# Turning the next block's query input by VectorE and DRAM transfers in place of TensorE, and two query products by halves of the tokens

## The reference

```python
x = x + jnp.tanh(g_xattn[0]) * xattn(_layernorm(x), ctx_1024, Wq, Wk, Wv, Wo)
x = x + jnp.tanh(g_ffn[0])   * ffn(_layernorm(x), W_r, W_k, W_v, mu_r, mu_k)
# xattn: Q = q @ Wq.T, K = c @ Wk.T, V = c @ Wv.T, softmax(Q K^T / sqrt(32)) V @ Wo.T
# ffn:   xr, xk = mixes of x and x of the token before; sigmoid(xr @ W_r.T) * (relu(xk @ W_k.T)**2 @ W_v.T)
```

## Time and profile before

| | us |
|---|---|
| median of 3 runs | 1389.31 |
| lowest and highest | 1386.89, 1389.38 |
| the profiled execution, its own time | 1387.71 |
| its span in the trace | 1386.0 |
| TensorE busy | 1349.9 |
| VectorE busy | 1037.6 |
| ScalarE busy | 779.3 |
| GpSimd busy | 598.7 |

### The profile page before, as it was taken

How to read it: one execution, slowest core, us unless ns; L and a number is a source line. 1 busy time by engine, 2 the same in 40 slices (tenths; PEclk the granted TensorE clock), 3 DMA queues, 4 the chain that set the end, 5 groups by cost and what they waited for, 6 DMA issues and landing times.

```text
span 1386.0 us, 28131 instructions
## 1 busy us (share of the span) xinstructions
PE 1349.9 (97%) x9484; PEld 989.5 (71%) x9484; DVE 1037.6 (75%) x1938; ACT 779.3 (56%) x1457; POOL 598.7 (43%) x802
## 2 busy tenths in 40 slices
PE   7999999999999999999999999999999999999998
PEld 5666776777767677776777767677776777767677
DVE  6777777786877868777786877868777786877763
ACT  7745637465473645637465473645737465473633
POOL 7524345353443535345353443525344343443534
PEclk9999999999999999999999999999999999999999
DMA  9421101212111121202112111121202112111011
GB/s 304 151 57 47 59 23 66 57 53 75 53 37 38 61 68 53 64 19 73 47 53 75 53 43 32 61 68 53 67 16 76 45 53 75 53 48 28 31 47 39
DMA packets 97563, 83.88 MB, mean 61 GB/s; under 512 B 47872, under 2 KB 62720, under 8 KB 97536
## 3 DMA queue, kind: packets, MB, share of 16 engines
q1 hardware_dynamic: 97536, 83.54, 19.6%
HBM read 57.75 MB, written 20.71 MB: 57 GB/s over the span
## 4 chain that ended last, share of the span: by engine, by line
PE 80%; ACT 9%; DVE 8%; issue 2%; DMA 0%; ACTq 0%; DVEq 0%
PE g_bank L1278 45%; PE g_bank L1441 7%; PE o_bank L1388 7%; PE s_bank L1362 4%; PE d_bank L1394 4%; ACT s_bank L722 3%; ACT pq L721 3%; PE s_bank L1338 3%; PE s_bank L1372 2%; PE d_bank L1284 2%; DVE buf L921 2%; ACT buf L627 2%; DVE o_bank L1065 1%; PE o_bank L1284 1%; DVE d_bank L1065 1%
## 5 line engine op out<-in xcount | busy, mean ns | idle before, releaser
L998 DVE TENSOR_TENSOR pq<-s_bank,pq 128x512 f16<-128x512 f32 x320 | 220.2, 688 | 72.0 <-ACT s_bank L722 71.2
L994 DVE TENSOR_REDUCE mm<-s_bank 128x3 f32<-128x462 f32 (+1 forms) x384 | 198.6, 576 | 89.0 <-PE s_bank L1338 89.0
L721 ACT ACTIVATE pq<-s_bank 128x512 f16<-128x512 f32 x320 | 192.3, 601 | 93.9 <-PE s_bank L1366 93.9
L1441 PE MATMUL g_bank<-buf,WkT 128*128 128x512 f32 x720 | 189.9, 410 | 5.7 <-DVE buf L921 4.0
L722 ACT ACTIVATE s_bank<-s_bank 128x512 f32<-128x512 f32 x320 | 194.7, 608 | 0.0
L1278 PE MATMUL g_bank<-xnT,WqT 128*128 128x512 f32 x756 | 194.4, 402 | 0.0
L1278 PE MATMUL g_bank<-WoT,buf 128*128 128x512 f32 x768 | 193.5, 401 | 0.0
L509 POOL TENSOR_TENSOR buf<-place,buf 128x512 fp32r<-128x512 f32 x64 | 82.7, 1293 | 235.7 <-ACT buf L627 235.7
L1278 PE MATMUL g_bank<-WrT,buf 128*128 128x512 f32 x744 | 184.1, 396 | 0.0
L1278 PE MATMUL g_bank<-WvT,buf 128*128 128x512 f32 x708 | 174.5, 395 | 0.0
L1278 PEld LDWEIGHTS g_bank<-WrT,buf 128*128 128x128 f32 x744 | 137.2, 188 | 39.7 <-issue 10.8
(11 more groups left out here) (168 smaller groups left out, 2121.8 us busy)
## 6 DMA issues: line engine op xcount, KB each, us to landing
xa<-in_x SPq DMA_DIRECT2D x64, 256.0 KB, 3.6
x<-in_x SPq DMA_DIRECT2D x64, 256.0 KB, 2.7
out<-x SPq DMA_DIRECT2D x48, 256.0 KB, 2.0
place<-x SPq DMA_DIRECT2D x16, 256.0 KB, 2.4
out<-place SPq DMA_DIRECT2D x16, 256.0 KB, 2.0
k_all<-k_scratch SPq DMA_DIRECT2D x15, 256.0 KB, 2.8
k_low<-k_scratch SPq DMA_DIRECT2D x15, 256.0 KB, 2.9
v_main<-v_scratch SPq DMA_DIRECT2D x15, 256.0 KB, 2.8
```

The lines of the kernel that those rows point to most:

```text
L721: nc.scalar.activation(pq[:, n, HI, :], bank[:, :], ACT.Exp, scale=SCALE).then_inc(p_hi, 1)
L994: nc.vector.reduce_max(maxima, scores, AX.X).then_inc(reduced, 1)
L998: nc.vector.tensor_tensor(pq[:, n, LO, :], score_bank[5 * g + n][:, :], pq[:, n, HI, :], ALU.subtract).then_inc(p_lo, 1)
L1441: ins = nc.tensor.matmul(K_BANK[c][:, :], WkT2[:, s, e, cols(c)], buf3[:, m, e, :], start=(e, n) == (0, 0), stop=(e, n) == (C - 1, len(PRO ...
```

## The change

For blocks 2 to 15, whose queries are made in the hardware loop, the turning leaves TensorE:

- SP loads block i+1 in four strips of 32 partitions (`load_strips`), so that a partition holds other tokens than before: the tokens that share a tile are now four runs of 32, 128 apart.
- ACT normalizes into a place of its own (`norm1_turn`, ahead of `tanh_r` of groups 1 and 2, before behind it), and DVE turns each tile in squares of 32x32 back into `xa` (`turn`, four instructions). The `gated` of group 2 moves behind that group's last `p_low`.
- SP stores two turned tiles to DRAM (`store_turned`, 512 KB) and loads them back with the squares in their places (`load_turned`, four transfers of 128 KB, in pieces of 256 bytes), for each half of the tokens. It waits for each store to land before the loads. Both halves stand on the one queue, the second store behind the first loads.
- ACT makes the high parts from SBUF in four instructions (`xT_high_half`) that stand behind the last `exps` of group 3 and ahead of `tanh_r(i - 1, 3)`. POOL makes three of the low parts (`xT_low_half`), DVE one (`xT_low_part`).
- `query(i + 1, 0)` and `query(i + 1, 1)` become `query_half`: first half of the tokens for both, then second half, 12 matmuls of 4x64 columns each time.
- `load_keys(i + 1)` moves ahead of two loads of `x1`.

Block 1 keeps the transposes of TensorE.

```diff
+            def load_strips(i):
+                for a in range(4):
+                    rows = slice(DH * a, DH * a + DH)
+                    sp.dma_start(xa[rows, :, :], x_strips[i, a]).then_inc(xa_loaded[a], 16)
+            def store_turned(i, h):
+                sp.wait_ge(xT_turned, i * TT - 2 + 2 * h)
+                sp.dma_start(xt_scratch[h], xa[:, 2 * h:2 * h + 2, :].rearrange("p t n -> p (t n)").rearrange("p (k n) -> p k n", n=2 * TAIL)).then_inc(xT_stored, 16)
+            def load_turned(i, h):
+                sp.wait_ge(xT_stored, i * 32 - 16 + 16 * h)
+                squares = xt_scratch[h].rearrange("(a r) (c b) n -> b r c a n", a=4, b=4)
+                for b in range(4):
+                    rows = slice(DH * b, DH * b + DH)
+                    sp.dma_start(xnT_loaded_part[rows, :, :, h, :], squares[b]).then_inc(xT_loaded[h], 16)
...
                 if ffn:
                     sp.wait_ge(x1_kept, 16 * i)
                     load_x1(i, TT - 1)
                     store_out(i - 1, 0)
+                    if pre:
+                        store_turned(i, 0)
+                        load_turned(i, 0)
+                        store_turned(i, 1)
                     store_out(i - 1, 1)
+                    if pre:
+                        load_turned(i, 1)
+                        load_keys(i + 1)
...
+            def xT_low_half(i, h, part):
+                chunks, n = slice(2 * part, 2 * part + 2), i * TT + 2 * h + part + 1
+                pool.wait_ge(xT_hi, n)
+                nc.gpsimd.tensor_tensor(xnT_part[LO][:, chunks, :, h, :], xnT_loaded_part[:, chunks, :, h, :],
+                                        xnT_part[HI][:, chunks, :, h, :].bitcast(F32), ALU.subtract).then_inc(xT_lo_pool, 1)
...
                     exps(i, g, 4)
+                    if ffn and pre:
+                        for t in ((0, 1), (2, 3), ())[g - 1]:
+                            norm1_turn(i + 1, t)
+                        if g == 3:
+                            for h in range(2):
+                                for part in range(2):
+                                    xT_high_half(i + 1, h, part)
                     if ffn:
                         tanh_r(i - 1, g)
...
+            def turn(i, t):
+                h = t // 2
+                dve.wait_ge(xn1_ready, i * TT + 2 * h + 2)
+                nc.vector.transpose(turned[h][:, :, t % 2, :], xn1[t % 2].rearrange("p (k s) -> p k s", s=TAIL)).then_inc(xT_turned, 1)
...
+            def query_half(i, g, h):
+                for n, (s, m) in enumerate(((HI, HI), (LO, HI), (HI, LO))):
+                    if m == LO and g == 0:
+                        pe.wait_ge(xT_lo_pool, 3 * i - 1 + h)
+                        if h:
+                            pe.wait_ge(xT_lo, i + 2 * TT)
+                    elif m == LO and h:
+                        maxima(i + 1, 0)
+                    for c in range(C):
+                        ins = nc.tensor.matmul(tokens_of(Q_BANK[g][:, :], h), WqT[:, s, c, cols(g)], tokens_of(xnT[:, m, c, :], h), start=(n, c) == (0, 0),
+                                               stop=(n, c) == (len(PRODUCTS) - 1, C - 1))
+                if h:
+                    ins.then_inc(q_done, 1)
...
-                if pre:
-                    xT(i + 1, 0, True)
...
+                if pre and ffn:
+                    for h in range(2):
+                        pe.wait_ge(xT_hi, (i + 1) * TT + 2 * h + 2)
+                        for g in range(2):
+                            if h == 0:
+                                pe.wait_ge((th_ready, u_ready)[g], i * TT)
+                            query_half(i, g, h)
```

More of the change, by code:

```diff
@@ L117, in flamingo_block @@
         xn2 = (xa[:, 0, :], xa[:, 1, :])
+        xn1 = (place[:, 6, :], place[:, 7, :])
+        turned = [xa[:, 2 * h:2 * h + 2, :].rearrange("p t n -> p (t n)").rearrange("p (k t s) -> p k t s", t=2, s=TAIL) for h in range(2)]
+        xnT_part = [xnT[:, n, :, :].rearrange("p c (a h n) -> p c a h n", a=4, h=2) for n in range(2)]
+        xnT_loaded_part = xnT_loaded.rearrange("p c (a h n) -> p c a h n", a=4, h=2)
         q32 = (xa[:, 2, :], xa[:, 3, :], xa[:, 2, :], xa[:, 3, :])
@@ L403, in step @@
                         sp.wait_ge(later_stored[n], LATER_STORES[n])
-                if pre:
+                if pre and not ffn:
                     load_keys(i + 1)
@@ L568, in step @@
                     attn_low(i, g - 1)
+                    if ffn and pre and g == 3:
+                        for h, part in ((0, 0), (0, 1), (1, 1)):
+                            xT_low_half(i + 1, h, part)
                     if ffn:
@@ L673, in _, with norm1_turn, xT_high_half, norm2 @@
                 norm1(0, t)
-            def norm2(i, t, pre):
+            def norm1_turn(i, t):
+                if t >= 2:
+                    act.wait_ge(xT_turned, (i - 2) * TT + 2)
+                act.wait_ge(norm_ready[0], i * TT + t + 1)
+                nc.scalar.activation(xn1[t % 2], xa[:, t, :], ACT.Identity, bias=nb[:, 0, t:t + 1],
+                                     scale=rstd[:, 0, t:t + 1]).then_inc(xn1_ready, 1)
+            def xT_high_half(i, h, part):
+                act.wait_ge(xT_loaded[h], (i - 1) * 64)
+                chunks = slice(2 * part, 2 * part + 2)
+                high(xnT_part[HI][:, chunks, :, h, :], xnT_loaded_part[:, chunks, :, h, :], xT_hi)
+            def norm2(i, t, turned):
                 if t >= 2:
                     act.wait_ge(x2_done, i * TT + t - 1)
-                elif pre:
+                elif not turned:
                     act.wait_ge(xT_done, (i + 1) * TT + t + 1)
@@ L693, in q_high, with q_copy, q_split @@
                 high(buf4[:, HI, g, :], Q_BANK[g][:, :], q_hi)
-            def q_copy(i, g, loop):
-                if g < 2:
+            def q_copy(i, g, turned):
+                if g < 2 and not turned:
                     act.wait_ge(xT_done, i * TT + g + 3)
-                else:
+                elif g >= 2:
                     act.wait_ge(q_lo, i * G + g - 1)
                 nc.scalar.activation(q32[g], Q_BANK[g][:, :], ACT.Copy).then_inc(q_copied, 1)
-            def q_split(i, g, loop):
+            def q_split(i, g, loop, turned=False):
                 q_high(i, g, loop)
-                q_copy(i, g, loop)
+                q_copy(i, g, turned)
             def k2_high(i, c):
@@ L819, in step @@
                         kv_high(KV_UNITS - 1)
-                    if pre and g == 3:
+                    if pre and not ffn and g == 3:
                         xT_high(i + 1, 0)
@@ L893, in _ @@
             end_k_high(0, 0)
[L894 removed]
+            norm2(LAST, 2, True)
             for c in range(1, C):
@@ L1508, in step @@
                     keys_or_values(FIRST_LATER + 1)
-                values(i, 0, pre)
+                values(i, 0, not ffn)
                 head_scores(i, 1)
@@ L1520, in step @@
                     keys_or_values(FIRST_LATER + 3)
-                values(i, 1, pre)
+                values(i, 1, not ffn)
                 head_scores(i, 2)
@@ L1532, in step @@
                     keys_or_values(FIRST_LATER + 5)
-                values(i, 2, pre)
+                values(i, 2, not ffn)
                 head_scores(i, 3)
@@ L1544, in step @@
                     ffn_v(i - 1, 2)
-                if pre:
+                else:
                     for t in range(1, TT):
-                        xT(i + 1, t, True)
-                values(i, 3, pre)
+                        xT(1, t)
+                values(i, 3, not ffn)
                 if not ffn:
```

100 lines of the change are left out of this document (59 added, 41 removed).

## The result

The changed kernel took 1398.68 us in the median (lowest 1390.4), the kernel before 1386.95 on the same chip: a ratio of 1.0075, with an interval of 1.0061 to 1.0089. It is slower by 0.75%, some 10 us (the two medians lie 11.7 apart), where 9 us less was foreseen. The profiled execution took 1402.15, with a span of 1399.2, and a mean granted clock of TensorE of 0.990 where before had 0.997. One of the 20 executions, 1618.44 us at a clock of 0.753, is left out of the ratio.

The account below looks back on a forecast made before the run. TensorE, busy for 97% of the span, was taken as the bound. Per step -1.74 + 0.7 + 0.18 + 0.1 + 0.1 = -0.66 us, in 14 steps -9.3, gave 1380 from a median of 1389.31; range 1367 to 1402.

Parts of the forecast that it names:

- Late through DRAM: Rival, chance 0.26: both stores and the last load, in series on one queue, land late; middle 1.3 us late, 1398.
- The work that leaves TensorE: Transposes in head group 3 of each loop step: 0.44 plus 1.30, a saving of 1.74 us a step.
- the halves with their waits: First two queries in halves: +0.18 us a step, plus 0.1 for waits within them and 0.1 for `maxima`.
- Where TensorE would wait and on what: Ahead of the first half query, 0.7 us a step, on `tanh_r` behind the high parts needing the second loads.
- the first store: Store of 512 KB of turned tiles: 2.8 us to landing, 0.2 more to wake SP for the loads.
- What was costed at nothing: DVE's turns, ACT's normalizations, POOL's low parts and the key loads in the step: hidden, no cost.
- The 0.2 for waits within the halves and of `maxima`: TensorE's waits per step: 0.1 us within the half queries and 0.1 for `maxima(i + 1, 0)`.
- Landed at 661.0: Second store of turned tiles, issued at 658.2 behind the first four loads, landed at 661.0 in the step's time.
- landed at 665.75: Last of the second loads, fourth issued at 663.15: 2.3 us plus 0.3 for 96 KB more at 330 GB/s.
- a rival at +0.2 a step: Within Late through DRAM (0.26): 256-byte pieces at half rate, last load 0.9 us later, +3 us, 1392.
- The rule that the prediction set against its sum: Skill's fixed 2.0 us plus bytes at 436 GB/s: store 3.2, load 2.3, chain 0.5 longer, sum -0.16 a step.
- Cutting the queries in halves doesn't help there: At TensorE's first half query: the second half's loads decide the start, since `tanh_r` stands behind all four high parts.

Follow-up runs that it names:

- tanh_first: The changed kernel with `tanh_r(i - 1, 3)` moved on ACT from behind the four high parts to ahead of them: 1365.13 us, ratio 0.9846.
- halves_only: The kernel before, with only the first two query products of the loop's blocks cut in halves of the tokens: 1390.71 us, ratio 1.003.
- out_behind: The changed kernel with the 256 KB output store on SP issued behind the second loads and not ahead of them: 1386.26 us, ratio 0.9991.
- pause_4: The kernel before with four extra copies of `tanh_r` of group 3 ahead of the real one, so that TensorE waits: 1419.04 us, ratio 1.0228.
- pause_6: The kernel before with six extra copies of `tanh_r` of group 3 ahead of the real one, so that TensorE waits: 1453.22 us, ratio 1.0474.

## Why the prediction was wrong

**Which rival came.** The time fell within the range, on the slower side. The case that came is *Late through DRAM*, near its middle: the transfers were some 1.2 us late where 1.3 was named. That its 1398 was met is in part luck: from a median of before of 1386.95 the waits alone give 1392, and the rest came from the clock, which the case did not have.

**Right.** The work that leaves TensorE, 1.74 us a step, and the halves with their waits, 0.18 to 0.28: `tanh_first` gives -1.56 and `halves_only` +0.23. Where TensorE would wait and on what. The turns (1.30 for two, 1.44 foreseen), the first store (2.64 to its loads, 3.0 foreseen) and four issues in 2.65. What was costed at nothing (DVE's turns, ACT's normalizations, POOL's parts, the keys) did cost nothing: in `tanh_first` nothing of it is left over. The 0.2 for waits within the halves and of `maxima` was not needed there either.

**The step that failed: "Landed at 661.0" and "landed at 665.75".** The second store and the last load were priced like transfers that run alone. From the second store's issue to its loads' there were 3.76 us in the mean and not 3.0, and from the last load's issue to its high part 3.8 and not 2.7 (the third high part starts 14.86 us after the first store in the mean; less 5.34, 3.76 and the 1.96 of three issues). That is 1.86 more; the first store gave back 0.36 and an earlier start some 0.4. So the wait was 0.7 + 1.1 = 1.8 (1.89 measured). Each of the two runs beside the transfers ahead of it: the store beside loads that keep the engines busy at 197 GB/s, the last load behind three others and the output (0.4 of it, by `out_behind`). The text had seen the small pieces at half rate, and kept them in a rival at +0.2 a step, for the last load alone. That the same half rate also lengthens the store behind them is what the windows of step 7 show. The rule that the prediction set against its sum, 3.2 us for a store, did not give this either: the Trainium skill, DMA: Bandwidth & Descriptors, "Anatomy of one DMA", states it for transfers that GpSimd issues, here SyncE issues them, and the first store let its loads go after 2.64.

**What was not in it at all: the clock.** With the waits alone the change costs -1.74 + 1.89 + 0.2 = +0.35 a step, 5 us, and the fastest executions, from 1390.4 up, are about that. In the profiled one the other 9 us are six stretches at 1.2 GHz. The loop of before could not have given the chance of them, since its TensorE is never idle for over 0.5 us. But the same trace shows the clock at 0.50 for 6.6 us in step 0, ahead of the loop, after two idle times of 1.33 and 1.49 us with 0.57 of work between them:

```profile
PE o_bank L1388 <- DVE pq L998: 6.4, 13, 0.5
...
114.06 0.57 PE L1338 MATMUL s_bank<-k_all,buf 32*128 32x154 f32 x12 [1.33 <-ACT buf L627]
116.12 8.53 PE L1441 MATMUL g_bank<-buf,WkT 128*128 128x512 f32 x24 [1.49 <-DVE buf L921]
...
115.40:122.00 6.60, 5.88 (x14) 4.64 (x15) 6.53 (x13) 1.79 (x3) 1.29 (x1) 0.50 0.17 49
```

(The first line is that of the longest idle times from 172 to 1250 us.) So that a wait can cost more than its length stood in the profile of before, and was the thing to ask. The Trainium skill, TensorE: Matmul & The Clock Gate, "Part 1: The HAM clock gate (the "warmup" mystery)", says that the clock has two levels and goes to the lower after idle time; the rows agree, with 1.00 and 0.50 in the windows shown.

**A remark of the text that was right and not followed.** "Cutting the queries in halves doesn't help there", since `tanh_r` stands behind all four high parts. That was the main thing in the change: with that one instruction in front, the same transfers and the same halves give 1365.1, some 33 us under the changed kernel and 22 under the one before.

**What stays open.** Why the clock falls after one wait of 1.87 us and not after the next of the same length; and how the second store's time divides between loads and output where both stand beside it.

## What to carry to other kernels

When a transfer is put in place of an engine's work, price it beside the transfers that its neighbours issue, not from a row in which it ran alone. A product cut in halves to run over a late transfer helps only if everything else that its first half waits for stands ahead of what needs that transfer, in each engine's order. A wait of 2 us on TensorE cost up to 3.5 here, and filling it with useless matmuls made the kernel faster. Look in the profile of before, outside the loop too, for what the clock did after idle time.

## What the runs showed of the hardware

The granted clock fell to 0.50 in kernels whose TensorE was busy for 95 to 96% of the span, after single waits of 1.87 to 3.12 us, more often after the longer: 3 of 14 steps at 1.87 (`pause_4`), 6 of the 8 steps with 1.99 to 2.46 in the changed kernel, 11 of 14 at 3.12 (`pause_6`). It did not fall after the one wait of 2.42 in `out_behind`. In step 0 of the kernel before it fell after two shorter ones close together, 1.33 and 1.49. Back at 2.4 GHz it was after 3.4 us, in 8 of the 11 steps of `pause_6` after some 6.8. Transfers of 256-byte pieces held the DMA engines 85% busy at 197 GB/s, and a store of 512 KB in long rows moved at 406. A second queue did not shorten a store that shared the engines: 4.05 us to its loads' issue in the mean against 3.76.
